# Attention output kept with its dimensions on partitions, up to its projection

## What is computed

```python
x = x + 0.5 * ffn(layernorm(x))
x = x + attention(layernorm(x))
x = x + 0.5 * ffn(layernorm(x))
# attention: 32 heads of 16 dimensions, 8 key/value heads, each for 4 query heads
q, k, v = bitnet_linear(x, q_weight), bitnet_linear(x, k_weight), bitnet_linear(x, v_weight)
scores = einsum('bhqd,bhkd->bhqk', q, k) / sqrt(16)
out = einsum('bhqk,bhkd->bhqd', softmax(scores), v)
return bitnet_linear(out, o_weight)     # y = x @ sign(w).T * (mean|w| * scale), nan_to_num
```

## Time and profile before

| what | value |
|---|---|
| median of 3 runs | 1157.1 us (1156.59 to 1159.24) |
| the profiled execution | 1159.3 us, of which its span 1157.5 us |
| mean granted TensorE clock | 0.967 |
| PE busy | 1076.3 us (93%) |
| DVE busy | 844.4 us (73%) |
| ACT busy | 727.1 us (63%) |
| GpSimd (POOL) busy | 293.3 us (25%) |
| moved by DMA | 59.42 MB, 17.6% of the engines' time |

### The profile page before, as it was taken

One profiled execution on the slowest core, in us unless ns is written; L12 is line 12 of the kernel. 1 busy time (PEld: TensorE's weight loads), 2 busy tenths in 40 slices (PEclk: granted clock), 3 DMA queues, 4 the chain that ended last, 5 costly groups with the idle time before them and its releaser, 6 DMA issues.

```text
span 1157.5 us, 16340 instructions
## 1 busy us (share of the span) xinstructions
PE 1076.3 (93%) x5968; PEld 484.5 (42%) x5968; DVE 844.4 (73%) x1146; ACT 727.1 (63%) x1361; POOL 293.3 (25%) x485
## 2 busy tenths in 40 slices
PE   5989887999999999999999999999999999998857
PEld 3778661344334433344334333433343334333436
DVE  5766679767776778877888678777977887782173
ACT  6457432757865787675776567666766675768420
POOL 5365556302510250410140014003200320041010
PEclk9989886999999999999999999999999999999979
...
DMA packets 87359, 59.42 MB, mean 51 GB/s; under 512 B 44144, under 2 KB 73328, under 8 KB 87280
## 3 DMA queue, kind: packets, MB, share of 16 engines
q1 hardware_dynamic: 87280, 58.39, 17.6%
...
## 4 chain that ended last, share of the span: by engine, by line
PE 74%; DVE 12%; ACT 6%; POOL 3%; issue 3%; DMA 1%; SPq 1%; DVEq 0%; POOLq 0%
PE ps_out L1452 20%; PE ps_score L1440 18%; PE ps_max L1415 16%; PE ps_fill L1373 5%; DVE neg_max L1218 3%; ACT probs L954 3%; PE ps_fill L1400 2%; PE ps_fill L1341 1%; PE ps_fill L1355 1%; PE ps_fill L1377 1%; DVE neg_max L1043 1%; DVE zd L1110 1%; PE ps_out L1373 1%; PE ps_max L1429 1%; PE ps_fill L1347 1%
## 5 line engine op out<-in xcount | busy, mean ns | idle before, releaser
L954 ACT ACTIVATE probs<-ps_score 128x512 f32<-128x512 f32 x992 | 539.0, 597 | 272.5 <-PE ps_score L1440 270.8
L1218 DVE TENSOR_REDUCE neg_max<-ps_max 128x1 f32<-128x1024 f32 x480 | 572.1, 1220 | 168.6 <-PE ps_max L1415 167.0
L1415 PE MATMUL ps_max<-kst,qst 96*128 96x512 bf16 x1024 | 294.0, 388 | 14.6 <-DVE neg_max L1043 5.7
L1440 PE MATMUL ps_score<-qst,kst 99*128 99x512 bf16 x992 | 305.1, 385 | 1.2 <-ACT probs L954 0.8
L1452 PE MATMUL ps_out<-probs,v_ring 128*32 128x512 f32 x2048 | 273.6, 606 | 8.1 <-ACT o_sb L960 5.3
L1440 PEld LDWEIGHTS ps_score<-qst,kst 99*128 99x128 bf16 x992 | 77.8, 97 | 254.3 <-ACT probs L954 210.0
L1415 PEld LDWEIGHTS ps_max<-kst,qst 96*128 96x128 bf16 x1024 | 88.4, 98 | 143.3 <-issue 17.6
L793 POOL CAST shift<-neg_max 128x16 bf16<-128x16 f32 x32 | 7.5, 236 | 463.3 <-DVE neg_max L1218 458.9
L1452 PEld LDWEIGHTS ps_out<-probs,v_ring 128*32 128x32 f32 x2048 | 41.0, 108 | 101.9 <-issue 92.0
L889 ACT ACTIVATE xn<-xc,ln_shift,rstd 128x512 f32<-128x512 f32 x48 | 38.5, 811 | 30.0 <-POOL ln_shift L690 19.0
L1373 PE MATMUL ps_fill<-wb_h,xt_h 128*128 128x512 f32 x84 | 46.9, 559 | 1.6 <-DVE xc L1205 0.8
...
## 6 DMA issues: line engine op xcount, KB each, us to landing
qst<-q_dram SPq DMA_DIRECT2D x192, 64.0 KB, 2.2
q_dram<-zm SPq DMA_DIRECT2D x24, 256.0 KB, 2.6
kst<-k_dram SPq DMA_DIRECT2D x192, 32.0 KB, 2.2
...
```

The source lines that it names most:

```text
L954: act.activation(probs[:, kt % 2, j, :], score_bank(i, uu, j), ACT.Exp, scale=1.0 / HD ** 0.5).then_inc(probs_ready, 1)
L1218: dve.tensor_reduce(neg_max[:, uu % 2, t:t + 1], ps_max[max_slot(uu, pos)][:, :, :], AXY, ALU.max, negate=True).then_inc(max_read, 1)
L1415: last = pe.matmul(ps_max[slot][:, half, :], qst[0:SR, r, j, q * P:(q + 1) * P], kst[0:SR, r, half * 512:half * 512 + 512], start=True, st ...
L1440: pe.matmul(score_bank(i, uu, j), kst[0:SR + PARTS, uu, kt * P:(kt + 1) * P], qst[0:SR + PARTS, uu, j, :], start=True, stop=True).then_inc ...
```

## The change

The transposes on both sides of `att_dram` go, and with them `normalise`. `o_sb` is stored as it is, outputs and sums (`att_dram` is now [block, head, partition, query]), in slot 1 of the next unit. A back chunk loads outputs and sums, dimensions on partitions, with eight DMAs: `att_t` (the memory of `xn`) holds four groups of 128 dimensions by 256 tokens, and `sum_t` (the memory of `zd`) for each of them the sum that belongs to it, repeated in 16 rows. For each of the two tiles of tokens, DVE inverts 4 x 128 columns of `sum_t` (NRa, NRb), multiplies (N0a, N0b), ACT copies to `xt_h`, and DVE subtracts (N0al, N0bl); the projection now waits for that subtraction. The last unit goes from `o_sb` into `att_t` and `sum_t` by 16 small DMAs (`load_last_out`). The line numbers in the changed kernel are 15 to 40 higher.

The core of the diff:

```diff
 BACK = [s.split() for s in (
-    12 * [""] + ["T0a", "T0al", "", "T0b", "T0bl", "", "Oa0", "Oa1", "C0", "Ob0", "Ob1", "", "G0 C1", "P0", "", "G1", "P1",
+    11 * [""] + ["NRa", "N0a", "N0al", "NRb", "N0b", "N0bl", "", "Oa0", "Oa1", "C0", "Ob0", "Ob1", "", "G0 C1", "P0", "", "G1", "P1",
...
-        att_dram = nc.dram_tensor("att_dram", [T // P, KV, P, REP * HD], F32, kind="Internal").ap()
+        att_dram = nc.dram_tensor("att_dram", [T // BLK, KV, P, BLK], F32, kind="Internal").ap()
...
+        att_t = [t[:, :, :].rearrange("p t d -> p (t d)").rearrange("p (c n) -> p c n", c=DC) for t in xn]
+        sum_t = [t[:, 0:DC * CH].rearrange("p (c n) -> p c n", c=DC) for t in zd]
...
+                for c in range(DC):
+                    kvs = 1 if ch.tail and c == DC - 1 else 2
+                    heads = att_dram[bass.ds(a // 2, 1), 2 * c:2 * c + kvs, :, (a % 2) * CH:(a % 2) * CH + CH].rearrange(
+                        "o k (j x) t -> (o k j) x t", x=2 * HD)
+                    for dst, rows in ((att_t[s], slice(0, HD)), (sum_t[s], slice(HD, 2 * HD))):
+                        sp.dma_start(dst[0:kvs * REP * HD, c, :], heads[:, rows, :]).then_inc(chunk_loaded[s], 16)
+
+            def load_last_out(ch):
+
+                s = ch.slot
+                sp.wait_ge(o_copied, NU)
+                for j in range(REP):
+                    to = slice(((KV - 1) % 2 * REP + j) * HD, ((KV - 1) % 2 * REP + j + 1) * HD)
+                    for dst, r0 in ((att_t[s], 32 * j), (sum_t[s], 32 * j + HD)):
+                        sp.dma_start(dst[to, DC - 1, :], o_sb[r0:r0 + HD, (NU - 1) % 2, s * CH:s * CH + CH]
+                                     ).then_inc(last_out_loaded[s], 16)

             def load_qk(i, uu):

...
                                  ).then_inc(rows_loaded[r], 16)

-            def store_att(i, uu, use):
+            def store_att(i, uu):

                 j = i + uu // UB
-                sp.wait_ge(max_read, use + 1)
-                sp.dma_start(att_dram[bass.ds((j // 2) * QT, QT), bass.ds((j % 2) * UB + uu % UB, 1), :, :]
-                             .rearrange("q o p d -> p q (o d)"), att[:, uu % 2, :, :]).then_inc(att_stored[uu % 2], 16)
+                sp.wait_ge(o_copied, i * UB + (uu + 1))
+                sp.dma_start(att_dram[bass.ds(j // 2, 1), bass.ds((j % 2) * UB + uu % UB, 1), :, :]
+                             .rearrange("o k p t -> (o k p) t"), o_sb[:, uu % 2, :]).then_inc(att_stored[uu % 2], 16)

             def body(i, plan, load_next, first=False, last=False):
                 for slot in range(8 * UB):
                         load_qk(i, uu + 3)
                     if kt == 2 and not (last and uu == 3):
                         load_rows(i, uu + 1, turn_use(i, uu, last))
-                    if kt == 4 and not (first and uu == 0):
-                        store_att(i, uu - 1, turn_use(i, uu, last))
+                    if kt == 1 and not (first and uu == 0):
+                        store_att(i, uu - 1)
                     if slot == 5 and load_next is not None:
                         load_x1(load_next, chunk_loaded[0])
...
             body(7, back_plan(ch), ch, last=True)
+            for ch in tail:
+                load_last_out(ch)
             load_x1(tail[0], x1_loaded[0])
             for item in tail_steps():
...
-                if pos in ("T0a", "T0b", "T1a", "T1b", "T2a", "T2b"):
+                if pos in ("N0a", "N0b"):
+                    t = 0 if pos.endswith("a") else 1
+                    act.wait_ge(att_normed[s], n * 2 + (t + 1))
+                    act.activation(xt_h[s][:, :, t * P:(t + 1) * P], att_t[s][:, :, t * P:(t + 1) * P],
+                                   ACT.Copy).then_inc(xt_h_ready[s], 1)
+                if pos in ("T1a", "T1b", "T2a", "T2b"):
                     t = 0 if pos.endswith("a") else 1
                     act.wait_ge(filler_ready[s], ch.written(pos))
...
                 act.wait_ge(probs_used, i * (8 * UB) + 8 * (uu + 1))
+                unit = UB * i + uu
+                if unit >= 2:
+                    act.wait_ge(att_stored[unit % 2], 16 * (unit // 2))
                 act.activation(o_sb[:, uu % 2, :], ps_out[:, :], ACT.Copy).then_inc(o_copied, 1)

             def body(i, plan, first=False):
...
                                           ALU.add).then_inc(bias_added[s], 1)
-                if pos in ("T0al", "T0bl", "T1al", "T1bl", "T2al", "T2bl") and not (ch.alone and ch.front):
+                if pos in ("NRa", "NRb"):
+                    tok = slice(0, P) if pos == "NRa" else slice(P, CH)
+                    dve.wait_ge(chunk_loaded[s], ch.load)
+                    if ch.tail:
+                        dve.wait_ge(last_out_loaded[s], 16 * 2 * REP)
+                    dve.reciprocal(sum_t[s][:, :, tok], sum_t[s][:, :, tok]).then_inc(recip_ready[s], 1)
+                if pos in ("N0a", "N0b"):
+                    t = 0 if pos == "N0a" else 1
+                    tok = slice(t * P, (t + 1) * P)
+                    dve.wait_ge(recip_ready[s], n * 2 + (t + 1))
+                    dve.tensor_tensor(att_t[s][:, :, tok], att_t[s][:, :, tok], sum_t[s][:, :, tok],
+                                      ALU.mult).then_inc(att_normed[s], 1)
+                if pos in ("N0al", "N0bl"):
+                    t = 0 if pos == "N0al" else 1
+                    tok = slice(t * P, (t + 1) * P)
+                    dve.wait_ge(xt_h_ready[s], ch.t0 + (t + 1))
+                    dve.tensor_tensor(xt_l[s][:, :, tok], att_t[s][:, :, tok], xt_h[s][:, :, tok].bitcast(F32),
+                                      ALU.subtract).then_inc(att_low_ready[s], 1)
+                if pos in ("T1al", "T1bl", "T2al", "T2bl") and not (ch.alone and ch.front):
                     stage = pos[:3]
                     bnk = ch.bank(stage)[0]
                     t = 0 if stage.endswith("a") else 1
...
-            def normalise(i, uu, use, slot):
-
-                k = uu % 2
-                o = ps_max[slot][:, 1, :].rearrange("p (q j n) -> p q j n", q=QT, j=REP)
-                dve.wait_ge(max_scores, use + 1)
-                dve.reciprocal(recip[:, k, :, :], o[:, :, :, HD]).then_inc(recip_ready, 1)
-                dve.wait_ge(recip_ready, i * UB + (uu + 1))
-                if isinstance(i, int) and UB * i + uu == NU - 1:
-
-                    for s in range(2):
-                        dve.tensor_tensor(xn[s][:, :, (KV - 1) * REP * HD:].rearrange("p q (j d) -> p q j d", j=REP),
-                                          o[:, s * CT:(s + 1) * CT, :, 0:HD],
-                                          recip[:, k, s * CT:(s + 1) * CT, :].unsqueeze(3).broadcast_to([P, CT, REP, HD]),
-                                          ALU.mult).then_inc(att_ready, 1)
-                    return
-                if not isinstance(i, int) or UB * i + uu >= 2:
-                    dve.wait_ge(att_stored[k], i * 32 + 16 * (uu // 2))
-                dve.tensor_tensor(att[:, k, :, :].rearrange("p q (j d) -> p q j d", j=REP), o[:, :, :, 0:HD],
-                                  recip[:, k, :, :].unsqueeze(3).broadcast_to([P, QT, REP, HD]),
-                                  ALU.mult).then_inc(max_read, 1)
+                                ).then_inc(max_read, 1)

...
-                if pos in ("T0a", "T0b", "T1a", "T1b", "T2a", "T2b"):
-                    if pos.startswith("T0"):
-                        pe.wait_ge(chunk_loaded[s], ch.load)
-                        if ch.tail:
-                            pe.wait_ge(att_ready, s + 1)
-                    else:
-                        which = 1 if pos.startswith("T2") else 0
-                        pe.wait_ge(xn_ready[s], ch.ln(which) * 2 + (t + 1))
+                if pos in ("T1a", "T1b", "T2a", "T2b"):
+                    which = 1 if pos.startswith("T2") else 0
+                    pe.wait_ge(xn_ready[s], ch.ln(which) * 2 + (t + 1))
...
                 if pos in ("Oa", "Ob"):
+                    if piece == 0:
+                        pe.wait_ge(att_low_ready[s], ch.n * 2 + (t + 1))
                     for c in (2 * piece, 2 * piece + 1):
...
-            def turn(i, uu, use, slot, rows=True, out=True):
+            def turn(i, uu, use, slot):

                 max_slot_free(use)
-                if rows:
-                    pe.wait_ge(shift_parts, i * (4 * UB) + 4 * (uu + 2))
-                    last = pe.transpose(ps_max[slot][:, 0, 0:P // 2].bitcast(BF16), shift[:, (uu + 1) % 2, :], identb[:, :])
-                if out:
-                    pe.wait_ge(o_copied, i * UB + uu)
-                    for q in range(QT):
-                        last = pe.transpose(ps_max[slot][:, 1, q * P:(q + 1) * P], o_sb[:, (uu - 1) % 2, q * P:(q + 1) * P],
-                                            ident[:, :])
-                last.then_inc(max_scores, 1)
+                pe.wait_ge(shift_parts, i * (4 * UB) + 4 * (uu + 2))
```

(11 more changed lines are left out.)

35 lines of the change are left out of this document (11 added, 24 removed).

## The result

| | before | changed |
|---|---|---|
| median | 1158.17 us (1156.59 to 1160.74, 4 runs) | **1219.49 us** (1217.93 to 1222.76, 4 runs) |
| profiled: span | 1157.5 us | 1218.0 us |
| profiled: mean granted clock | 0.967 | 0.933 |

The ratio is 1.0531, 95% interval 1.05 to 1.0561: slower by 61 us. The forecast was 1212, its range 1180 to 1250.

What follows compares the result with a forecast made beforehand. PE, busy for 93% of the span, was taken as the bound, with short leads over DVE and ACT. Against the profiled 1159.3, -14.0 removed + 57 loop + 12 tail = +55, 1214; as median 1212, range 1180 to 1250.

Steps and rivals of the forecast that it cites:

- Two short leads decide this case: Attention loop: PE may run ahead of DVE by two `ps_max` buffers and of ACT by two score banks, no more.
- The price of the reciprocal: DVE's 128x512 reciprocal: 2.82 us, from 5.2 ns a column and a fixed part of 0.155 us.
- The walk through the chunk: Loop chunk: PE pauses of 3.6 and 2.5 us, slot 9 7.5 us later; with the clock 9.5 a chunk, +57.
- What was removed: Transposes in `turn`: 31 x 0.45 = 14.0 us, all on PE's path; DVE's small reciprocal and multiply valued at nothing.
- The clock: Loop chunks: granted clock falls at the two pauses, adding 2.0 us a chunk, between 0 and 4.
- SyncE's queue: Eight attention loads at 0.52 us an issue, landed by 558.5 to 561.2, hidden with 1.3 to 4 us to spare.
- The tail: After the last unit: projection 5 us late, DVE's queue the bound, +12 in all.
- The pauses come, the clock stays up: Rival for the loop: pauses without a clock fall, -14 + 45 + 12 = +43, 1200; chance 0.17.
- dear column, small fixed part: Rival on the reciprocal: 5.2 us for 512 columns, +92.5, 1250; chance 0.14.
- no more than a copy: Rival on the reciprocal: it costs 0.68 us, -14 + 19 + 3 = +8, 1165; chance 0.04.
- loads come late: Rival on SyncE's loads: landing beyond 562.47 delays every chunk; at 3 us late +18, 1230; chance 0.05.
- faster: Rival for the loop: DVE's idle 168.6 us takes the new work, no pauses form, 1150; chance 0.05.

Runs made afterwards that it cites:

- experiment 1: Changed kernel with the wide reciprocal replaced by a multiply by a constant, output not normalised: 1170.46 us.
- experiment 3: Changed kernel with ACT's copies three half slots later and DVE's subtractions four half slots later in the loop: 1210.3 us.
- experiment 9: Kernel with compact sums, each inverted once per unit, but ACT's copy back in the same half slot as DVE's multiply: 1165.68 us.
- experiment 4: Changed kernel with the four transposes of `o_sb` per unit put back into `turn`, nobody reading them: 1232.75 us.
- version 8: Changed kernel with sums gathered compactly and inverted once per unit, multiplies and ACT's copies later, `o_sb` store earlier, own semaphore for `x1`: 1150.86 us.
- experiment 6: Changed kernel with the attention loads issued ahead of `x1`'s load, and `x1` given its own semaphore: 1223.1 us.
- experiment 7: Changed kernel with attention loads ahead of `x1`, own semaphore for `x1`, and all chunk loads meant to come a slot earlier: 1224.12 us.

## Why the prediction was right, and where its steps were off

**The bound.** "Two short leads decide this case" held. PE's waits for ACT before scores rose from 0.8 to 34.1 us, and experiments 1, 3 and 9 each moved them and the time the same way; in experiment 3 most of what ACT's lead gave back came up again at DVE's.

**The price of the reciprocal failed, by 0.53 us.** The prediction drew a line through the rows of 2 and 16 columns, 5.2 ns a column. The runs have 1747 ns for 256 and 3347 for 512: 1600/256 = 6.25 ns a column, and 3347 - 512 x 6.25 = 147 ns fixed. This line gives 247 and 160 ns for the two narrow rows, which were 239 and 166. They lie 8 and 6 ns off it, in opposite directions; stretched from 14 columns to 512 that became half a microsecond. The prediction's sum, with two uses in each of six chunks and three to four on the tail's path, moves by 12 x 0.53 = 6.4 us in the loop and by 1.6 to 2.1 us in the tail. With the measured price it would have read 1220, and 1219.5 was measured. That this is so close is luck in part: as the next paragraphs show, other terms were off by some us each and cancelled.

The Trainium skill ("VectorE: DVE Perf Modes", the walkthrough of the 8-slice pipeline) was read there as eight cycles a column at 0.96 GHz, 4.4 us. The page gives no time for a column. The trace disagrees with that reading: 6.25 ns is six cycles at that clock.

**The walk through the chunk** was right in order and kind. Forecast: pauses of 3.6 us before scores and 2.5 before `ps_max` and scores; found in the chunk shown: 4.06, and 0.68 + 1.13 = 1.81. The "twelve idle times of 2 to 4 us" came as six of 3.7 to 5.2 and twelve shorter ones, and PE's busy share as 89% instead of 86 to 88%. Loop in all: +57 - 14 = +43 forecast, +46.0 found. With the measured gain per unit, 0.51, the chunks' share is (46.0 + 31 x 0.51)/6 = 10.3 us each, where 9.5 was forecast; 1.06 for the two dearer reciprocals would have made it 10.6.

**What was removed** came out near its sum, with a wrong cause. 0.45 us a unit was forecast, all of it PE's transposes, and 0.51 is found on average in the 19 units named above. But "all on PE's path, since PE has no idle time there" holds for ten of these units and not for nine, by experiment 4, and "PE did not wait for DVE there, so I value this at nothing" was wrong too: the trace of the kernel before has such a wait, 1.00 us in unit 4, and with the transposes back 5.4 of the 9.8 us are still there. The transposes were priced too high here and DVE's small work too low, and the two cancelled: this is luck.

**The clock.** It fell twice a chunk, behind the pauses, as forecast, and its mean over the unit with the chunk and the one behind it is 0.92 in all six, where it was 1.00 before. Measured as matmul time, its share was set too low, and that of the waits was set too high. The walk's 7.5 us later, with the 0.88 us of transposes that were gone, needed 8.4 us more of idle time on PE a chunk; the twelve units have 36.8 us more than before, 6.1 a chunk. The clock was put at 2.0 us a chunk, between 0 and 4; the same matmuls take 27.8 us longer than in version 8, 4.6 a chunk. This is no clean price of the clock, since with faster matmuls PE would have waited longer in places, but the two errors stand against each other.

**SyncE's queue failed in its margin.** "Hidden with 1.3 to 4 us to spare" was wrong. The issue took 0.58 to 0.66 us, not 0.52; the first one came at 558.28, 6.1 us later than in the earlier trace rows, while DVE asked 4.8 us later; and the last landing took 4.70, near the upper end taken from the earlier trace rows. In the chunk shown the data came just when asked for, and in all DVE waited 3.7 us in five waits. A wait of DVE for these loads was one of the prediction's signs of being wrong, and it came. It was no main cause: in experiment 1 DVE waits 3.5 us for the same loads, and 49 us of the loss are gone. What the 3.7 us themselves cost is not shown, since experiments 6 and 7 did not remove them.

**The tail** was forecast at +12 and is +14.5; the order of its pieces on DVE was as walked, and the reciprocal's price accounts for 1.6 to 2.1 of the 2.5.

**The rivals.** "The pauses come, the clock stays up" is excluded by the windows; "dear column, small fixed part" by the 147 ns and by 3.35 us against 5.2 (its sum is 92.2, not 92.5, on which nothing hangs); "no more than a copy" by the same row, and its 1165 is near the 1170.5 of experiment 1, where the pass does cost no more; "loads come late" as a case of some 18 us by DVE's waits for them, 3.7 us in all, and by experiment 1; "faster" by six chunks of +8.5 us. DVE's 168.6 us of idle time in the earlier trace rows was no cover: it is 180.3 now, with all the new work done, since it lies in gaps between reductions while the new work comes in one piece.
